# Low parts of the shared experts on VectorE, and router logits with the tokens held as weights

## The reference, cut to what matters

```python
x = x + 0.5 * L0_ffn(layernorm(x)); x = x + L0_attn(layernorm(x)); x = x + 0.5 * L0_ffn(layernorm(x))
# the same for L1, L2 and L3, each with its own mixer and experts

# L1 (L3 alike, with a sigmoid gate on the shared part, which is four times as wide; L2: gelu, not gated, 16 experts)
probs = softmax(xf @ gate_w.T)                 # the router: 8 or 16 columns
topk_p, topk_i = top_k(probs, 2)               # two experts a token
h = silu(einsum('nc,eic->eni', xf, w1)) * einsum('nc,eic->eni', xf, w2)
y = einsum('enc,ne->nc', einsum('eni,eci->enc', h, w3), comb)
y = y + (silu(xf @ sw1.T) * (xf @ sw2.T)) @ sw3.T      # the shared expert: every token

# L0: gate_logits = xf @ gate_w + expert_bias (7 columns), sigmoid, top 2, and a capacity of int(T / 7) tokens an expert
```

## Time and profile before

| | |
|---|---|
| median of three runs | 3240.19 us (3236.42 to 3241.41) |
| the profiled execution's own time | 3237.12 us |
| its span in the profile | 3235.3 us |
| TensorE products busy | 2859.1 us, 88% |
| VectorE busy | 2223.7 us, 69% |
| ScalarE busy | 1503.0 us, 46% |
| GpSimd busy | 1531.7 us, 47% |
| chain that ended last | PE 67%, DVE 17%, ACT 5%, DMA 4%, issue 3%, POOL 3% |
| mean granted clock of TensorE | 0.924 of full |

### The profile page before, as it was taken

The page is one execution under the profiler, slowest core; times in us unless marked ns, Lnnn a source line. Parts: engine busy times, 40 slices in busy tenths (PEclk is TensorE's granted clock), DMA queues, the critical chain, the costliest instruction groups (busy, mean ns, idle before and its releaser), DMA issues.

```text
span 3235.3 us, 60360 instructions
## 1 busy us (share of the span) xinstructions
PE 2859.1 (88%) x20922; PEld 2556.8 (79%) x20922; DVE 2223.7 (69%) x6068; ACT 1503.0 (46%) x3245; POOL 1531.7 (47%) x1493
## 2 busy tenths in 40 slices
PE   8979999999999899896698987769997858976898
PEld 6869999999999888795487876757776847966697
DVE  6767777777777767665735667568886765664665
ACT  3355666656666533344523434445454534443342
POOL 2345565655555405635600445658884545350134
PEclk9989999999999899897798987979998978989899
DMA  4022222222212210363004343810002553650533
GB/s 152 1 70 73 56 58 65 56 73 56 73 52 70 89 41 5 102 212 130 20 0 152 115 125 109 251 37 2 2 2 72 185 139 83 194 193 0 215 95 105
DMA packets 147766, 285.81 MB, mean 88 GB/s; under 512 B 20673, under 2 KB 70209, under 8 KB 144385
## 3 DMA queue, kind: packets, MB, share of 16 engines
q1 hardware_dynamic: 113458, 211.38, 19.8%
q0 software_dynamic: 21216, 57.96, 6.8%
q10 hardware_dynamic: 12816, 12.78, 1.2%
HBM read 191.59 MB, written 90.45 MB: 87 GB/s over the span
## 4 chain that ended last, share of the span: by engine, by line
PE 67%; DVE 17%; ACT 5%; DMA 4%; issue 3%; POOL 3%; SPq 0%; DVEq 0%; ACTq 0%; POOLq 0%
PE bank L552 17%; PE bank L553 17%; PE bank L554 17%; PE bank L2555 3%; PE bank L2571 2%; PE bank L1292 2%; DMA MXG<-dxn,IDX 2%; PE bank L1005 1%; DMA YG<-dyo,POSI 1%; POOL YG L1750 1%; PE bank L692 1%; PE bank L1314 1%; PE bank L723 1%; DVE ST L603 1%; PE bank L1211 1%
## 5 line engine op out<-in xcount | busy, mean ns | idle before, releaser
L1738 POOL DMA_INDIRECT MXG<-dxn,IDX x250 | 237.4, 949 | 248.7 <-PE bank L1292 211.8
L1750 POOL DMA_INDIRECT YG<-dyo,POSI x192 | 187.2, 975 | 177.1 <-DMA dyo<-YS 106.3
L2702 POOL TENSOR_SCALAR SX<-SX,MN 128x256 f32<-128x256 f32 x256 | 233.8, 930 | 46.1 <-DVE MN L2633 46.0
L1581 POOL TENSOR_TENSOR SHL<-SGS,SHH 128x512 fp32r<-128x512 f32 x18 | 25.0, 1391 | 391.1 <-ACT SHH L1386 391.1
L2633 DVE CUSTOM_DVE_ANT_0 SX<-bank,FMASK 128x128 f32<-128x128 f32 (+1 forms) x512 | 156.2, 351 | 48.0 <-PE bank L2546 47.9
L1104 POOL TENSOR_TENSOR HL<-HID,HH 128x512 fp32r<-128x512 f32 x56 | 72.4, 1292 | 240.3 <-ACT HH L1069 240.1
L552 PE MATMUL bank<-MWH,GH 128*128 x500 | 170.7, 341 | 0.7 <-DVE HB L1655 0.6
L1422 ACT ACTIVATE GH<-bank 128x256 fp32r<-128x256 f32 x250 | 95.6, 384 | 141.2 <-PE bank L1292 140.5
L552 PE MATMUL bank<-MWH,SHH 128*128 128x256 f32 x352 | 108.8, 309 | 53.8 <-DVE SHL L1581 27.6
L554 PE MATMUL bank<-MWH,GL 128*128 x500 | 154.8, 310 | 0.0
L553 PE MATMUL bank<-MWL,GH 128*128 x500 | 154.7, 309 | 0.0
(11 more groups left out here) (464 smaller groups left out, 11586.1 us busy)
## 6 DMA issues: line engine op xcount, KB each, us to landing
dyo<-YS SPq DMA_DIRECT2D x250, 128.0 KB
RAW<-in_wheads SPq DMA_DIRECT2D x68, 320.0 KB, 6.1
BB<-dgates SPq DMA_DIRECT2D x68, 256.0 KB, 3.6
GB<-dgates SPq DMA_DIRECT2D x68, 256.0 KB, 4.4
RAW<-in_eL SPq DMA_DIRECT2D x32, 304.0 KB, 2.9
dkeptL<-MWL SPq DMA_DIRECT2D x32, 304.0 KB
dkeptL<-MWH SPq DMA_DIRECT2D x32, 304.0 KB
MWH<-dkeptL SPq DMA_DIRECT2D x8, 1216.0 KB, 12.7
```

Source lines behind the costliest of these rows:

```text
L1738: nc.gpsimd.indirect_dma_start(MXG[:, n % XGS, :], None, dxn, bass.IndirectOffsetOnAxis(ap=IDX[:, b:b + 1], axis=0)).then_inc(x_in[n % XGS ...
L1750: nc.gpsimd.indirect_dma_start(YG[:, i % YGS, :], None, dyo[0:m.blocks * P, :], bass.IndirectOffsetOnAxis(ap=POSI[:, c * NT + t:c * NT + t ...
L2702: nc.gpsimd.tensor_scalar(part, part, MN[:, n % RING2, 1:2], None, ALU.subtract).then_inc(s_less1, 1)
```

## The change

Four edits go together.

1. The logits are made with the tokens held. For each tile of 128 tokens four products (two halves of the features by high and low part of x) have XTH or XTL as weights, 128 x 128, and stream 32 or 16 columns of RWS. They give for each token 32 columns: 16 by the high part of the router's weights (and the low part of x by the same), and 16 by the low part. ScalarE's copy and the products with HALVES are gone. VectorE adds the two halves: in L0 by one more add, in a moe stage by a COPY and an ADD ahead of MAX8 (which now reads SBUF); the subtraction comes last, with a semaphore of its own (r_shift). The bank is free for the next group (r_tops) once the halves are added, and the wait for it now stands ahead of the group's products. In a tailed front sums and top two stand one slot earlier.
2. Every early low part SHL is made by VectorE, in the gated stages between the first two and the last one-hot of a chunk; in moe:L2 the first before the places' last part (moe_slots), the others one step ahead. GpSimd makes none.
3. The inverse products of chunks 2 and 3 come later: gated after up(5) (with the index and the expert offsets behind the low part of step 4), not gated after down(4), and chunks 0 and 1 after up(4).
4. The 24 products after the early steps are dropped in the gated stages and are 8 in moe:L2.

**VectorE, early steps of the first moe:L1 stage.** Rows of the order, before: SGS is the multiply of a step, SHL its low part, HOT, AHOT and BHOT a chunk's one-hots, X the shared expert's result added, IDX the list.

```diff
-        RWS = main.put('RWS', [P, 4, KC, 64], F32R)
-        HALVES = main.put('HALVES', [32, 16])
+        RWS = main.put('RWS', [P, 4, KC, 32], F32R)
...
         def front_tensor(pe, st):
...
                 if st.routed and 2 <= g < GROUPS:
                     moe_logits(pe, st, 2 * g - 4)
                     moe_logits(pe, st, 2 * g - 3)
-                if st.routed and 3 <= g < GROUPS:
-                    logits_sum(pe, st, 2 * g - 6)
-                    logits_sum(pe, st, 2 * g - 5)
...
                 if st.routed and g >= GROUPS:
-                    logits_sum(pe, st, 2 * g - 6)
-                    logits_sum(pe, st, 2 * g - 5)
                     moe_logits(pe, st, 2 * g - 4)
                     moe_logits(pe, st, 2 * g - 3)
-            if st.routed:
-                logits_sum(pe, st, HALF - 2)
-                logits_sum(pe, st, HALF - 1)
...
         def route0_vector(dve, st):
             dve.wait_ge(r_logits, HALF * (st.rt + 1))
-            nc.vector.tensor_tensor(LG[:, :, 0:8], bank[4][:, 0:NT * 16].rearrange('p (t e) -> p t e', e=16)[:, :, 0:8],
-                                    EB[:, :].unsqueeze(1).to_broadcast([P, NT, 8]), ALU.add).then_inc(l0_made, 1)
+            one, other = both_halves(LOGIT, slice(0, NT), 8)
+            step(nc.vector.tensor_tensor(LG[:, :, 0:8], one, EB[:, :].unsqueeze(1).to_broadcast([P, NT, 8]), ALU.add))
+            nc.vector.tensor_tensor(LG[:, :, 0:8], other, LG[:, :, 0:8], ALU.add).then_inc(l0_made, 1)
...
-        INVERSE_AT = {True: (3, 4), False: (3, 5)}
-
-        def low_by_pool(st, s):
-
-            return s < LOWS_BY_VECTOR + 2 and (st.cached or s >= LOWS_BY_VECTOR)
+        INVERSE_AT = {True: 3, False: 4}
...
         def moe_logits(pe, st, p):
 
             pe.wait_ge(xt_lo, st.tr * HALF + p + 1)
-            if p >= 2:
-                pe.wait_ge(lg_sb, HALF * st.rt + p - 1)
-            o = bank[p % 2][0:32, 0:2 * P]
-            for k in range(KC):
-                x = slice(p * 2 * P, (p + 1) * 2 * P)
-                nc.tensor.matmul(o, RWS[:, st.router, k, 0:32], XTH[:, k, x], start=k == 0, stop=False)
-                last = nc.tensor.matmul(o, RWS[:, st.router, k, 32:64], XTL[:, k, x], start=False, stop=k == KC - 1)
-            last.then_inc(logits, 1)
-
-        def logits_sum(pe, st, p):
-
-            pe.wait_ge(lg_sb, HALF * st.rt + p + 1)
             g = p // 2
             if st.kind == 'moe' and p % 2 == 0 and g >= 2:
                 pe.wait_ge(r_tops, GROUPS * st.moe + g - 1)
-            o = bank[LOGITS[g % 2] if st.kind == 'moe' else LOGIT]
-            for q in range(2):
-                t = 2 * p + q
-                last = nc.tensor.matmul(o[:, t * 16:(t + 1) * 16], LGS[:, p % 2, q * P:(q + 1) * P], HALVES[:, :],
-                                        start=True, stop=True)
+            b = LOGITS[g % 2] if st.kind == 'moe' else LOGIT
+            for t in (2 * p, 2 * p + 1):
+                for k in range(KC):
+                    hi, lo = xt(k, t * P, P)
+                    nc.tensor.matmul(bank[b][:, t * 32:(t + 1) * 32], hi, RWS[:, st.router, k, :], start=k == 0, stop=False)
+                    last = nc.tensor.matmul(bank[b][:, t * 32:t * 32 + 16], lo, RWS[:, st.router, k, 0:16], start=False, stop=k == KC - 1)
             last.then_inc(r_logits, 1)
...
+        def both_halves(b, tiles, E):
+
+            o = bank[b][:, :].rearrange('p (t h e) -> p t h e', h=2, e=16)[:, tiles]
+            return o[:, :, 0, 0:E], o[:, :, 1, 0:E]
...
             for s in range(m.early):
                 shared_up(pe, st, s, moe_prefix if s == 0 else None)
-                if s in INVERSE_AT[m.gated]:
-                    n = 2 * INVERSE_AT[m.gated].index(s)
-                    moe_inverse(pe, st, n)
-                    moe_inverse(pe, st, n + 1)
+                if s == INVERSE_AT[m.gated]:
+                    moe_inverse(pe, st, 0)
+                    moe_inverse(pe, st, 1)
+                if s == 5 and m.gated:
+                    moe_inverse(pe, st, 2)
+                    moe_inverse(pe, st, 3)
                 if s:
                     shared_down(pe, st, s - 1)
+                if s == 5 and not m.gated:
+                    moe_inverse(pe, st, 2)
+                    moe_inverse(pe, st, 3)
             shared_down(pe, st, m.early - 1)
-            warm(24, 1)
+            if not m.gated:
+                warm(8, 1)
...
         def moe_tops(dve, st, g):
...
             dve.wait_ge(r_logits, HALF * st.rt + 2 * g + 2)
+            one, other = both_halves(LOGITS[g % 2], part, wide)
+            step(nc.vector.tensor_copy(ML1[:, part, 0:wide], one))
+            nc.vector.tensor_tensor(ML1[:, part, 0:wide], other, ML1[:, part, 0:wide], ALU.add).then_inc(r_tops, 1)
+            dve.wait_ge(r_tops, GROUPS * st.moe + g + 1)
             for t in tiles:
-                last = nc.vector.max(TOP[:, t, :], o[:, t, 0:E])
+                last = nc.vector.max(TOP[:, t, :], ML1[:, t, 0:E])
             step(last)
...
             for s in range(m.early):
+                c = s if s < 4 else None
                 shared_product(dve, st, s)
-                if not low_by_pool(st, s):
-                    shared_low(dve, nc.vector, st, s)
...
-                if s < 2:
-                    moe_hot(dve, st, s)
-                if s == 2:
-                    if m.J == 2:
-                        shared_add(dve, st, 0)
-                    moe_hot(dve, st, 2)
-                    moe_hot(dve, st, 3)
-                if s == 3 and m.J == 3:
-                    shared_add(dve, st, 0)
-                if s == (4 if m.gated else 5):
+                if c is not None:
+                    moe_block_hot(dve, st, c)
+                if s == 4 and not m.gated:
                     moe_index(dve, st)
+                if s + (not m.gated) < m.early:
+                    shared_low(dve, st, s + (not m.gated))
+                if s == 4:
+                    if m.gated:
+                        moe_index(dve, st)
                     moe_experts(dve, st)
-                if s > 3 and s % m.J == 0:
+                if m.J == 3 and s == 3 or m.J == 2 and s in (1, 3):
+                    shared_add(dve, st, (s + 1) // m.J - 1)
+                if c is not None:
+                    moe_slot_hot(dve, st, c)
+                if m.J > 3 and s and s % m.J == 0:
                     shared_add(dve, st, s // m.J - 1)
...
         def moe_pool(pool, st):
...
             for s in range(m.early):
-                if low_by_pool(st, s):
-                    shared_low(pool, nc.gpsimd, st, s)
                 if st.tailed:
                     pieces_low(pool, st, pieces_by(m, s), pieces_by(m, s + 1))
```

More of the change, by code:

```diff
@@ L1347, in moe_tensor @@
             nx = st.next
[L1348 removed]
+            for k in range(m.front_of(GROUPS - 1) + (4 if nx else 1)):
                 for g in range(GROUPS if nx else 0):
@@ L1456, in moe_scalar @@
                         front_high(act, nx, 2 * g + 1)
-                    if k == done + 3 and nx.kind == 'moe':
-                        logits_high(act, nx, 2 * g)
-                        logits_high(act, nx, 2 * g + 1)
                     if k == done + 1:
```

71 lines of the change are left out of this document (27 added, 44 removed).

## The result

The changed kernel took 3252.86 us (median of six, 3246.79 to 3256.52) against 3237.71 (six, 3232.32 to 3241.41): ratio 1.0044, interval 1.0034 to 1.0055. It is 15 us slower where 10 faster was forecast. Its profiled execution took 3256.52 us, its slowest, span 3254.7.

What follows compares the result with a forecast made beforehand. TensorE was taken to bound the kernel (67% of the chain, VectorE 17%). Router +0.6, moe:L1 -3.6, moe:L3 -4.8, moe:L2 -3.5 sum to -11.3 us: 3225.8 from 3237.1, 3227 as a median, range 3213 to 3240.

Steps and rivals of the forecast that it cites:

- The router in the moe fronts: Four moe stages with their own front: new products, a wait and added VectorE steps cost +0.9 us each, +3.6 in all.
- The router in the tailed fronts: Two tailed fronts, among block and shared work TensorE can do: 0, bounds -0.7 and +1 us for half of either.
- L0's fronts: Router in L0: only the last 16 products follow the last low part; -2.0 us first stage, -1.0 second.
- The rival of slow thin products: Router products take 0.28 us each in place of 0.13, +33 us, 3260; +18 from 0.08 more per product; chance 0.10.
- moe:L2, first stage: Without GpSimd's low parts ahead of its weight pieces everything moves up 3.2 us; taken as -3.0 (-3.4 to -1).
- moe:L2, second stage: 16 of 24 idle products go, but the list is about 1.5 us late and gathers follow it: -0.5 (-2 to +2).
- Gated early steps: Low parts on VectorE, idle products dropped: moe:L1 -1.8 us a stage; moe:L3 second stage -3.3, first -1.5.
- Clock rival: Dropped idle products and thin new ones leave the clock low at ups and first blocks: 3237; 0.25 together with undone gains.
- The last rival: Late list or VectorE's longer row hurts more in moe:L2 and moe:L1: within 0.2%; 0.25 together with the clock rival.

Runs made afterwards that it cites:

- e5: The kernel before with the router's part of the change alone, every other buffer kept at its old address: ratio 1.0042 to the kernel before, 3246.62 us.
- e8: e5 with four banks instead of two for the logits of moe fronts that aren't tailed: ratio 1.0000 to the kernel before, 3234.33 us.
- e7: e6 with the new router in L0's two fronts alone, in the same buffers: ratio 0.9999 to the kernel before.
- e6: The kernel before with the changed early steps in the gated stages alone, without their idle products; moe:L2 and router as before: ratio 0.9999.
- e11: The kernel before with the changed early steps in moe:L2 alone, with 8 idle products there; gated stages and router as before: ratio 1.0031.
- e4: The changed kernel with 24 idle products after the early steps of all six moe stages: ratio 1.0038 to the kernel before, against 1.0044.
- e12: e6 with the 24 idle products back in the gated stages: ratio 0.9995 to the kernel before, against 0.9999.
- e15: The kernel before with four banks, new router, changed gated early steps and the changed kernel's buffer addresses; moe:L2's steps as before: ratio 1.0006.

## Why the prediction was wrong

- **The router in the moe fronts**, +0.9 a stage and +3.6 in all. The mechanism stood in the prediction: the wait ahead of the products, the low clock behind it, VectorE's added steps. It was mis-sized: XTL to MM rose by 1.2, 2.1, 1.3 and 0.8 us in the changed kernel's trace, about 5.4, and the whole router's part measured 13.5, of which 12 go with the two-bank wait (e5 against e8). I ended the front's account at the pick of the experts; from XTL to YG the two traces differ by the whole 12, as far as single traces show it. I also took the clock between its two levels where three of the four fronts had the low one for all 32 products and the fourth for 20 of 31 distances, and counted the wait as a start time alone, though the clock is low more often behind it (e8).
- **The router in the tailed fronts**, 0 with +1 as bound: the front of moe:L3 lost 3.3 us, outside the bound, and the stage gave it back.
- **L0's fronts**, -3.0: from XTL to the bias add the first took 3.1 us less and the second 1.8, and each lost 0.3, so about as worked out. Of the 3.1 a part is the low clock of the trace before (its second trace had 3.78 and not 5.15). As part of a median it isn't seen (e7 against e6).
- **The rival of slow thin products** (0.28 us each): its mechanism was wrong, though the time, 26 us above the forecast, lies between its +18 and +33. They follow one another at 0.11 and 0.21 us, and the bound of 0.13 and 0.23 from the sum's row was near. The Trainium skill's page "TensorE: Matmul & The Clock Gate", section "LDWEIGHTS (loading the stationary operand)", puts a load at its columns divided by 1.2 GHz, an estimate of 107 ns for 128; the trace agrees at the full clock (0.11) and not at the low one (0.21), and the 32 or 16 streamed columns count for nothing beside it.
- **moe:L2, first stage**, -3.0: the step that failed most. It held that without the two low parts "everything moves up 3.2". I took GpSimd's list as a chain of its own. It hangs on ScalarE's high parts of the weights, these stand between shared steps, and the shared steps now hung on VectorE's places and one-hots, stretched beside GpSimd: the last piece is done 2.8 us later behind the pick and the first block starts 5.6 us later, 4.0 in e11. The stretch was in the prediction for GpSimd's low parts and not for its weight pieces, which are the larger load: the earlier trace rows has 14.07 us of them in one row.
- The Trainium skill's page "GPSIMD Engine Reference", section "Key points", has VectorE and GpSimd share their interfaces to SBUF; it holds here with a price: HOT 1.55 against 0.55.
- **moe:L2, second stage**, -0.5 (-2 to +2): the list came 4.8 later behind XTL, not 1.5, since low parts, X and BHOT stand ahead of the inverse products as well, and the blocks behind gathers took 3.4 longer in e11. About +6 there, outside the bounds.
- **Gated early steps**, -1.8 a stage of moe:L1 and -3.3 in the second of moe:L3: the waits came as forecast. In e6's trace XTL to block of moe:L3 second is 5.1 us shorter, that of moe:L3 first 2.5 (forecast 1.5) and that of moe:L1 second 2.3 (0.4 in e7); for moe:L1 first the traces decide nothing (e11). Counted against a median: 0 (e6), and no run shows where it is given back. In the changed kernel the blocks of moe:L3 second took 3.2 longer (87.8 to 91.05), in e6 only 0.7. The sum for this stage was slightly off too: -1.0, +0.5 and -2.6 make -3.1.
- **Clock rival**: TensorE's clock was low behind the two-bank wait. The dropped idle products are worth nothing that can be told, alone (e4, e12) or beside four banks (0.9983 against 0.9995, with intervals that overlap), but all three pairs lean the same way, to the kernel that has them.
- **The last rival**, the late list or VectorE's longer row, named moe:L2 and came true there, but was held to 0.2%; it measured 0.31% alone (e11).
- **Sum of the parts**: 13.5 + 10 + 0 against 14 measured. Not settled: by the four kernels under e15 the two costs may overlap, and by the intervals they may also simply add.

## What to carry to other kernels

Before an operation is moved to an engine because that engine is idle in the trace, follow what every other engine's list hangs on behind it: here ScalarE's weight work stood between the steps that got later. Follow a front to the end of its stage, too, and not only to the next landmark. Put a wait where the waiting engine has work behind it that doesn't need it; in the changed kernel a 2 us pause stood ahead of 32 short products, and in three of four fronts all of them then ran at half the clock. When a buffer's reuse forces an order, look for an unused bank first.
